# Twelve of sixteen input tiles loaded by indirect gathers from GpSimd instead of two SyncE transfers

## What is computed

```python
mod = (_silu(L0_c) @ L0_wmod).reshape(L0_c.shape[0], 6, 1, -1)
sa, ca, ga, sb, cb, gb = (mod[:, 0], mod[:, 1], mod[:, 2], mod[:, 3], mod[:, 4], mod[:, 5])
...
h = _layernorm(x, axis=-1) * (1 + ca) + sa
x = x + ga * _L0_attn_ref(h, ...)      # qkv = silu(h @ w_qkv.T), and so on
```

## Time and profile before

| | us |
|---|---|
| median of 3 runs | 719.01 (717.83 to 719.47) |
| span of the profiled execution, first to last instruction | 715.6 |
| profiled execution, its own time | not recorded apart from the span |
| PE busy in the span | 668.4 (93%) |
| POOL busy in the span | 211.9 (30%) |
| first matmul of the QKV loop (L804) starts at | 19.02 |

### The profile page before, as it was taken

How to read it: one execution, slowest core, us unless ns; L and a number is a source line. 1 busy time by engine, 2 the same in 40 slices (tenths; PEclk the granted TensorE clock), 3 DMA queues, 4 the chain that set the end, 5 groups by cost and what they waited for, 6 DMA issues and landing times.

```text
span 715.6 us, 11552 instructions
## 1 busy us (share of the span) xinstructions
PE 668.4 (93%) x4132; PEld 570.2 (80%) x4132; DVE 482.1 (67%) x958; ACT 347.5 (49%) x758; POOL 211.9 (30%) x210
## 2 busy tenths in 40 slices
PE   3989889779998799999999999999999999999997
PEld 2768779769997588877888888888888888888885
DVE  3787788959997378767545766566655666655555
ACT  2367669869998984573223232232322322323222
POOL 1345767954018665214200340012200321000000
PEclk9989999979999799999999999999999999999999
DMA  8000000011000000023002331224321332122223
GB/s 313 1 0 1 1 1 1 1 65 48 3 2 2 1 1 0 1 93 105 25 29 82 103 118 60 71 82 126 85 72 65 111 115 84 61 64 60 69 72 120
DMA packets 20472, 41.48 MB, mean 58 GB/s; under 512 B 3360, under 2 KB 3616, under 8 KB 20288
## 3 DMA queue, kind: packets, MB, share of 16 engines
q1 hardware_dynamic: 19392, 37.65, 16.7%
q10 hardware_dynamic: 832, 2.43, 0.9%
q0 software_dynamic: 192, 0.66, 0.2%
HBM read 38.50 MB, written 2.23 MB: 57 GB/s over the span
## 4 chain that ended last, share of the span: by engine, by line
PE 73%; ACT 9%; DVE 8%; POOL 3%; issue 3%; DMA 3%; ACTq 0%; DVEq 0%; POOLq 0%
PE ps L970 36%; PE ps L1041 18%; ACT junk L634 3%; PE ps L804 2%; PE ps L909 2%; PE ps L910 2%; PE ps L898 2%; PE ps L834 2%; PE ps L885 2%; DMA qkvw<-in_qkvw 2%; PE ps L921 1%; ACT junk L584 1%; PE ps L988 1%; PE ps L1007 1%; DVE sq L1155 1%
## 5 line engine op out<-in xcount | busy, mean ns | idle before, releaser
L705 ACT ACTIVATE sgm<-ps,zero 128x512 f32<-128x512 f32 x100 | 68.9, 690 | 273.1 <-PE ps L970 273.1
L970 PE MATMUL ps<-h2hi,whi 128*128 128x512 f32 x400 | 156.1, 390 | 0.0
L970 PE MATMUL ps<-h2lo,whi 128*128 128x512 f32 x400 | 155.7, 389 | 0.0
L970 PE MATMUL ps<-h2hi,wlo 128*128 128x512 f32 x400 | 155.6, 389 | 0.0
L1446 DVE TENSOR_TENSOR am<-sgm,ps 128x512 f32<-128x512 f32 x88 | 60.5, 688 | 136.9 <-ACT sgm L705 136.8
L447 POOL CAST whi<-raw 128x768 fp32r<-128x768 f32 x25 | 22.0, 879 | 237.1 <-DMA raw<-in_moew 235.8
L970 PEld LDWEIGHTS ps<-h2lo,whi 128*128 128x128 f32 x400 | 75.1, 188 | 15.6
L970 PEld LDWEIGHTS ps<-h2hi,whi 128*128 128x128 f32 x400 | 75.1, 188 | 15.6
L970 PEld LDWEIGHTS ps<-h2hi,wlo 128*128 128x128 f32 x400 | 75.1, 188 | 15.4
L1041 PE MATMUL ps<-ahi,whi 128*128 128x512 f32 x200 | 77.9, 390 | 0.1
L1041 PE MATMUL ps<-ahi,wlo 128*128 128x512 f32 x200 | 77.8, 389 | 0.0
(11 more groups left out here) (204 smaller groups left out, 1244.8 us busy)
## 6 DMA issues: line engine op xcount, KB each, us to landing
raw<-in_moew SPq DMA_DIRECT2D x25, 384.0 KB, 3.9
cw<-combine SPq DMA_DIRECT2D x32, 256.0 KB, 3.2
cw<-combine SPq DMA_DIRECT2D x16, 224.0 KB, 3.0
cw<-combine SPq DMA_DIRECT2D x16, 192.0 KB, 2.8
cw<-combine SPq DMA_DIRECT2D x16, 160.0 KB, 2.7
cw<-combine SPq DMA_DIRECT2D x16, 128.0 KB, 2.9
out<-x1T SPq DMA_DIRECT2D x8, 256.0 KB, 3.6
cw<-combine SPq DMA_DIRECT2D x16, 96.0 KB, 2.7
```

Source lines behind the costliest of these rows:

```text
L705: ac.activation(sgm[:, n % 2, :], gate_bank(n), ACT.Silu, bias=zero[:, :]).then_inc(S["e_sg"], 1)
L970: last = mm(o, w_, a_[:, kc, tok], start=(kc == 0 and k == 0), stop=(kc == KC - 1 and k == 2))
```

## The change

x tiles 4 to 15 are no longer loaded by two plain transfers from SP. POOL first writes a table of row numbers (`rowid`, value 16 p + t, by iota), waits for it, and then issues twelve indirect gathers, one for each tile, each of 128 rows of 1 KB (128 KB). Its three old transfers follow behind the gathers. The first four gathers count on `ld_xb`, the other eight on `ld_xc`, and DVE waits for the full counts. The data that arrives is the same.

```diff
@@ -171,6 +171,7 @@
+        rowid = sb("rowid", [P, NT], mybir.dt.uint32)
@@ -314,8 +315,6 @@
             sp.dma_start(cT[:, :, :], c_d).then_inc(S["ld_c"], 16)
             sp.dma_start(x[:, 0:4, :], x_d[:, 0:4, :]).then_inc(S["ld_xa"], 16)
-            sp.dma_start(x[:, 4:8, :], x_d[:, 4:8, :]).then_inc(S["ld_xb"], 16)
-            sp.dma_start(x[:, 8:, :], x_d[:, 8:, :]).then_inc(S["ld_xc"], 16)
             sp.dma_start(w02[:, :, :], w02_d).then_inc(S["ld_w"], 16)
@@ -356,6 +355,11 @@
         @block.gpsimd
         def _(po):
+            po.iota(rowid[:, :], [[1, NT]], base=0, channel_multiplier=NT).then_inc(S["rowid"], 1)
+            po.wait_ge(S["rowid"], 1)
+            for t in range(4, NT):
+                po.indirect_dma_start(x[:, t, :], None, x_d.rearrange("p t d -> (p t) d"),
+                                      bass.IndirectOffsetOnAxis(ap=rowid[:, t:t + 1], axis=0)).then_inc(S["ld_xb" if t < 8 else "ld_xc"], 16)
             po.dma_start(wnat[:, :, :], wnat_d).then_inc(S["ld_wn"], 16)
@@ -1140,9 +1144,9 @@
-            ve.wait_ge(S["ld_xb"], 16)
+            ve.wait_ge(S["ld_xb"], 16 * 4)
             stats(1)
-            ve.wait_ge(S["ld_xc"], 16)
+            ve.wait_ge(S["ld_xc"], 16 * 8)
             stats(2)
```

More of the change, by code:

```diff
@@ L229, in build @@
         S = {n: sem(n) for n in (
-            "ld_xa", "ld_xb", "ld_xc", "ld_mod", "ld_mod2", "ld_id", "ld_qkv", "ld_c", "ld_wn", "ld_w", "ld_raw0", "ld_raw1", "st_out",
+            "rowid", "ld_xa", "ld_xb", "ld_xc", "ld_mod", "ld_mod2", "ld_id", "ld_qkv", "ld_c", "ld_wn", "ld_w", "ld_raw0", "ld_raw1", "st_out",
             "const", "silu_c", "mod_ps", "mod_sb", "mod_ok", "ohot_ok", "ga_ps", "ga_sb", "ga_ok", "wo_ok", "gb_ps", "gb_done", "wn_ss", "wn_ok",
```

## The result

The changed kernel takes 725.92 us (median of 3 runs, 722.85 to 727.8) against 719.01 before: a ratio of 1.0105, 95% interval 1.0074 to 1.0137. It is slower, by 6.9 us between the medians (0.96%; the ratio, which is not that of the medians, says a little more), inside the range of 717.0 to 731.0 and 3.2 us above the forecast of 722.7. The profiled execution has a span of 724.0 us, 8.4 more than the 715.6 before.

A forecast was written before the change was run, and what follows sets the result against it. The chain through qkvw's transfer, h1T and PE's QKV loop bounds the kernel; POOL's queue moves rstd to 16.6, plus 6.15 puts L804 at 22.76, 3.7 us later: span 719.3 plus 3.4 gives 722.7 us, range 717.0 to 731.0.

The forecast's parts named there:

- The place and the sign: Ahead of the QKV loop: POOL's queue delays rstd beyond its slack, L804 starts 3.7 us later; slower, chance 0.75.
- the relief of qkvw: Less traffic ahead of qkvw's transfer: it lands earlier, gaining at most 2.8 us, counted in full only if POOL is in time.
- The break-even: First rstd on POOL: L804 stays at 19.02 if rstd starts by 12.87, 3.85 us after its present start.
- The way from rstd to L804: From rstd's start through xn, transposes and h1T to the first QKV matmul: 6.15 us.
- twelve gathers: Issue time on POOL ahead of rstd: 1.1 us each, 13.2 us together, 6.5 and 22.3 at the bounds.
- The iota: Added on POOL ahead of the gathers: 0.24 us, bounds 0.10 and 1.86, plus 0.05 for its semaphore wait.
- D: Rival: gathers' data late, DVE waits at stats(2), costing only what exceeds 2 us of slack; no chance of its own.
- The 3.4 us around the span: Time outside the profiled span, added to the predicted span of 719.3 us to give 722.7 us.
- The clock allowance: PE's QKV tiles: one changing clock level moves the time by 1.7 us either way; two allowed.
- A: Rival: a gather on POOL costs about a plain transfer, 0.56 us; L804 at 16.2 at best, 716.2 us; chance 0.12.
- B: Rival: gathers on POOL cost 1.4 to 1.9 us each, adding 7.3 to 12.9 us, 726.3 to 731.9; chance 0.15.
- C: Rival: library selection ahead of the iota on POOL costs up to 5.9 us uncovered, up to 728.6 us; chance 0.15.

The follow-up runs named there:

- 10.84: Changed kernel with six gathers instead of twelve, tiles 4 to 9 by one plain SP transfer; rstd at 10.84; ratio to before 1.0003.
- 16.64: Changed kernel with POOL's own three transfers (wnat, woT, onw) issued by SP; rstd at 16.64; ratio to before 1.0081.
- 11.98 with x on SP: Kernel before, x still loaded by SP, plus iota and twelve unused 64-byte-row gathers on POOL; one execution, qkvw landed at 11.98, L804 at 24.66.

## Why the prediction was right

**The place and the sign: right.** The change uses up the slack of rstd on POOL and then delays L804, and the relief of qkvw is hidden behind it. The break-even was put at rstd's start of 12.87. The runs bracket it: at 10.84 nothing was lost, at 16.64 it was 3.9 us. The way from rstd to L804, summed to 6.15 us, measured 6.30 (18.34 to 24.64), and 6.30 and 6.26 in the kernels with 10.84 and 16.64.

**The term that was mis-sized: twelve gathers.** I priced one at 1.1 us, twice a plain issue; it measures 1.25 at a pace of 0.95 busy and 0.30 idle. All twelve, with what the first costs more, took 15.02 us (1.64 to 16.66) where the sum had 13.42. That is 1.6 of the 1.9 us by which L804 came later than forecast (24.64, not 22.76). The reason that I gave for the size was wrong: 128 rows, indices and addresses. The three plain transfers that I had read all have 128 rows, so they could not tell a price of the rows from a fixed one. With 64 rows a gather still takes 0.90, so it is nearly all a price of the instruction. That twice the plain price came within 0.15 us was therefore luck in part; no row gave the factor of two. The upper bound of 1.86 and the lower of 0.54 both held.

**The rest of the sum.** The iota took 0.14, not 0.24, but began at 0.84 and not at 1.24, and the first gather followed 0.67 us after it, not 0.05; together they nearly cancel (1.64, against 1.53). The first gather cost 0.30 more than the others, not 0.22. The three plain transfers took 1.68, not 1.66. qkvlo and stats fell as forecast, the gathers' data was never waited for in the changed kernel, and D did not occur there. qkvw landed earlier (11.06), as forecast, but the forecast credited x alone; that POOL's own 640 KB came later was left out as a relief, and the runs above show it to be one (11.98 with x on SP, and 8.91 against 10.69). Since that branch is hidden, the time does not hang on it. The 3.4 us around the span compare a median with another execution's span; wherever both are on record for one execution they are 1.8 to 2.5 us apart. The forecast of 722.7 keeps its value, since it is the median plus 3.7.

**From L804 to the time.** 5.6 us became 6.9 between the medians in the first timing and 6.5 in the second. The forecast passed the shift on one to one; the intervals allow that and lean to a little more. So of the 3.2 us by which the time lies above the forecast 1.9 are the later L804, and the rest is not explained. The clock allowance of 1.7 us a tile rested on a wrong reading: the twelve matmuls at 19.02 took 3.81 us at a granted clock of 1.00 (19.02 to 22.83), so this is not the price of the lower level, and no run here gives that price by itself. What single executions do differ by is larger, 4.7 us behind L804 in the unchanged kernel.

**The rivals.** A, the gather that costs like a plain transfer: it doesn't, but the experiment with plain transfers shows that its branch was put together well (rstd 9.51 against 10.1, L804 16.86 against 16.2 at best), except that even then the time does not measurably move: 0.9988 of before, where 716.2 would be 0.9961. B (1.4 and more a gather) did not occur. C, the library selection: the iota started at 0.84 and the first gather at 1.64, with no idle stretch over 0.67 us ahead of it, so it costs little if anything. The 6 us of the Trainium skill's "GPSIMD Engine Reference", section 2.1, for a first call appear in no run here. The rule weighed above, of the Trainium skill's "DMA: Bandwidth & Descriptors", section "Issuing engines are not separate DMA queues", says that issuing is usually small beside the transfer. Twelve gathers held POOL for 15.0 us (1.64 to 16.66), for 1.5 MB that the 400 GB/s seen on the full DMA engines move in under 4. For gathers of 128 KB the trace speaks against it, where many stand in a row; one gather's 1.25 us is small beside the 6.0 us (median) from its issue to its landing.

## What to carry to other kernels

Before moving a load to an engine that also computes, add its issue time up to the first thing that this engine owes to others, and compare it with the slack of that thing, found from its consumers back. A gather from GpSimd cost about 1.25 us of that engine's time here, with rows of 64 bytes to 4 KB, so make few and wide ones, or put the urgent operation ahead of them. If a load is late because others run beside it, hold those back with a wait on a queue that has nothing urgent: here this made the first L804 2.85 us sooner, without a gather, and the kernel 0.25% faster by an interval that just leaves 1 out.

## What the runs showed of the hardware that was not expected

- An indirect gather takes 0.95 us on POOL with 128 rows of 1 KB, 0.95 with 128 rows of 64 bytes, 0.94 with 128 rows of 4 KB, and 0.90 with 64 rows; 0.30 us stay idle behind each if another gather follows, and none if a plain transfer does. Plain transfers follow each other at 0.55.
- One gather beside a DVE subtraction of two SBUF operands took 2.21 us, once; that the one causes the other was not tested.
- What is issued beside a transfer moves its landing by microseconds: qkvw (774 KB), always issued at about 2.1, landed at 14.54 and 14.94 in the unchanged kernel, at 10.69 with 1.5 MB of x held back, and at 8.91 with POOL's 640 KB held back too.
- Beside gathers of 64 rows the DMA engines were as full as ever (share 1.03) and moved 285 GB/s from 9 to 11 us, against 387 beside gathers of 128 rows; one execution, and why is open.
- Two executions of one unchanged program differ by 5 us in span, with 24 narrow matmuls at 2.58 or 4.92 us, at a granted clock of 1.00 beside them in both.
